# Three buffers in place of two for the split queries between two attention layers

## Chip, cores and metric

The kernel runs on one core of one Trainium2 chip, as one program of 22310 instructions on five engines. TensorE (PE in the profile, its weight loads PEld) multiplies, VectorE (DVE), ScalarE (ACT) and GpSimd (POOL) do elementwise work, SyncE (SP) issues nearly all DMAs. The metric is the device time of one execution in microseconds, the median of several; lower is better.

## What is computed

Two transformer layers on x of shape 4 x 1024 x 128, in float32:

```python
x = L0_attn_query
xn = _layernorm(x)
x = x + _L0_attn_ref(xn, ...) + _L0_ffn_ref(xn, ...)   # causal attention, 16 heads of 8
xn = _layernorm(x)
x = x + _L1_attn_ref(xn, ...) + _L1_ffn_ref(xn, ...)   # keys strided by 3; 2 of 8 experts
```

What matters here lies between the two attentions. Layer 1 needs q = xn @ Wq.T for all 4096 tokens, and k and v of 342 compressed keys of each of the four batches, where a key is a convolution over three tokens of xn:

```python
kc = conv(x.transpose(0, 2, 1), Wconv, stride 3)
k_tmp = concatenate([x[:, :1, :], kc], axis=1)
q = x @ Wq.T;  k = k_tmp @ Wk.T;  v = k_tmp @ Wv.T
```

The router of the experts (the two best of eight, a sigmoid of xn @ gate_w) is computed in the same stage.

## The kernel before

The program is a row of blocks with a barrier of all engines after each: the first projection, a quantised feed-forward, attention of layer 0, `between_layers` (L1400), attention of layer 1, and the experts. The change lies in `between_layers`, with two places in its neighbours.

Scores are computed in bf16 at float32 accuracy: q and k are each split into three bf16 parts (a head, a middle, a tail) that add up to the float32 value. The tokens go through `between_layers` in eight chunks of 512, n = 0 to 7, two to a batch b = n // 2. For one chunk:

- TensorE turns the normalised rows (`turn_xn`, L1511), ScalarE copies them out of PSUM (`copy_xn`, L1616), TensorE projects them into the bank p_q[n % 2] (`query`, L1518) and computes the router's logits (`route`, L1529).
- ScalarE writes the head (`head_q`, L1622) to q_parts[n % 2][:, 0]; TensorE takes it off the bank (`take_off_q`, L1536); ScalarE writes the middle and, after another take-off, the tail (`rest_q`, L1626). The three parts of a chunk stay in one SBUF buffer, `q1_kept0` for even n and `q1_kept1` for odd n.
- SyncE stores the three parts to DRAM by three DMAs of 128 KB (`store_q1`, L1378, by `store_parts`, L202). Each adds 16 to the semaphore q_stored0 or q_stored1. `head_q(n)` waits at L1621 until the store of chunk n - 2, the last user of its buffer, has landed.

For each batch, once its second chunk is there, TensorE convolves (`convolve`, L1550), ScalarE copies the result (L1632), TensorE projects keys and values (`keys_values`, L1560 and L1564), and ScalarE splits the keys likewise: `head_k_copy_v` (L1639, L1642, L1646) and `rest_k` (L1651). The keys have one buffer, `k1_kept`: `head_k_copy_v(b)` waits at L1638 for the store of batch b - 1.

The order on each engine is written out by hand, in ten steps i = 0 to 9 (L1582 on TensorE, L1657 on ScalarE, L1770 on VectorE). ScalarE's step i holds, in this order: the copy of xn of chunk i; for even i from 2 on, the router's sigmoid; the middle of chunk i - 1; for even i, the copy of the convolution of batch i/2 - 1; for odd i from 3 on, the middle of that batch's keys; the head of chunk i; the tail of chunk i - 1; for even i, the head of the keys and the copies of v; for odd i, the tail of the keys. An engine runs its list strictly in order, so a wait holds back all that is listed behind it.

SyncE's list (L1470) is: stores of chunks 0, 1, keys 0, chunk 2, then a wait for keys 0 and chunks 0 and 1 in DRAM (L1480 to L1482) and half of the operand loads of head group 0 for the next attention (`load_operands`, L213 to L217, six or seven DMAs), store of chunk 3, the other half, keys 1, chunks 4 and 5, first half of group 1, keys 2, chunk 6, second half of group 1. The stores of chunk 7 and keys 3 are issued at the start of the next attention (L1015, L1016), which then waits for all of them (L1018, L1019).

At the end of the stage TensorE ranks the tokens of each expert (`rank`, 33 matmuls, L1573 and L1577), behind all else on its list, and VectorE computes from it the place of each token (`place_tokens`, L1734 to L1767). Then comes the barrier, at L1407.

The semaphores of COUNTS (L74) are each raised by one at the start of the program, by TensorE (`prime`, L114, called at L466 to L468).

Of the kernel before, what the change touches and what calls it, by code (L numbers as in the profile page):

```python
# [23 lines left out]
ACT = mybir.ActivationFunctionType  # L24
F32 = mybir.dt.float32
BF16 = mybir.dt.bfloat16
# [5 lines left out]
P = 128  # L32
B, T, E = 4, 1024, 128
H, D = 16, 8
TILES = B * T // P
CHUNK = 512
CHUNKS = B * T // CHUNK
# [9 lines left out]
PARTS = 3  # L47
# [14 lines left out]
START = 1  # L62
# [20 lines left out]
        exp_done unseen_zeroed pv_done v_staged o_copied inverse_done""",  # L83
    "between": """
        o_turned ot_copied projected x_added stats_done moment_steps root_steps xn_ready xn_turned xnt_copied
        q_projected heads_done rests_done middles_done tails_done q_stored0 q_stored1 logits_done conv_done conv_copied
        k_projected k_heads_done k_rests_done k_middles_done k_tails_done k_stored v_projected v_copied
        router_steps sigmoid_done""",
    "plan": """
# [98 lines left out]
Q_ORDER, K_ORDER = range(PARTS), range(PARTS - 1, -1, -1)  # L188
# [5 lines left out]
STORES = 16 * PARTS  # L194


def store_parts(sp, where, order, parts, first, count, stored):


    for row, part in enumerate(order):  # L200
        dst = where[:, row, :, :, bass.ds(first, count)].rearrange("g d a t -> g (d a) t")
        sp.dma_start(dst, parts[:, part, :]).then_inc(stored, 16)  # L202
# [714 lines left out]
def counted_before(layer):  # L917

    geo = Geometry(0)
    units = B * GROUPS  # L920
    uses = sum(what in BANK_USES for what, *_ in geo.order())
    layer0 = dict(banks_filled=uses, banks_read=uses, split_steps=units * geo.split, maxima_stored=16 * units, scores_t_ready=2 * units * geo.S,
                  exp_done=2 * units * geo.S, unseen_zeroed=2 * units * len(geo.masked), pv_done=units * geo.S,
                  v_staged=units, o_copied=units, inverse_done=units)
    return {name: START + layer * count for name, count in layer0.items()}
# [13 lines left out]
def attention(nc, io, sb, dram, layer):  # L939
# [4 lines left out]
    with ExitStack() as ctx:  # L944
# [16 lines left out]
        s, since = sb["counts"]["attention"], counted_before(layer)  # L961
# [23 lines left out]
        def read(use):  # L985

            return since["banks_read"] + use + 1

        def raw_load(sp, b, i):

            sp.wait_ge(e["cut_done"], START + 2 * (BATCH_CUTS * b + max(0, i - 1)))
            sp.dma_start(raw[i % 2][:, :], io["wraw"][b * BATCH_CUTS + i, :, :])\
                .then_inc(sb["raw_in"][i % 2], 16)

        def cut_store(sp, b, i):

            sp.wait_ge(e["cut_done"], START + 2 * (BATCH_CUTS * b + i + 1))
            where = dram["weights"][b * BATCH_CUTS + i, :, :]
            sp.dma_start(where, parts[i % 2][:, :, :].rearrange("p a h -> p (a h)").bitcast(F32)).then_inc(e[f"cut_stored{i % 2}"], 16)
# [12 lines left out]
        @block.sync  # L1012
        def _(sp):
            if layer == 1:
                store_q1(sp, sb, dram, B - 1, 1)  # L1015
                store_k1(sp, sb, dram, B - 1)  # L1016
                for par in range(2):
                    sp.wait_ge(sb["counts"]["between"][f"q_stored{par}"], START + STORES * CHUNKS // 2)  # L1018
                sp.wait_ge(sb["counts"]["between"]["k_stored"], START + STORES * B)  # L1019
            use = 0  # L1020
            for what, n, k, part in order:
                if what == "end" and layer == 0 and n < (B - 1) * GROUPS:
                    b, ends = n // GROUPS, n % GROUPS * 2 + k
                    if 2 <= ends < 2 + BATCH_CUTS:
                        cut_store(sp, b, ends - 2)
                    for i in {0: (0, 1)}.get(ends, (ends,)):
                        if i < BATCH_CUTS and ends != 1:
                            raw_load(sp, b, i)
                if what == "turn_max":
                    sp.wait_ge(s["banks_read"], read(use))  # L1030

                    sp.dma_start(sb["qp"][n % GROUPS][KROWS:FIRST, :, :].rearrange("r j t -> r (j t)"), top_rows[:, :])                        .then_inc(s["maxima_stored"], 16)
                    if layer == 1 and n + 2 < GROUPS:
                        load_operands(sp, sb, dram, layer, geo.keys, 0, n + 2)
                    if layer == 0 and n == B * GROUPS - 1:
                        sp.wait_ge(drawn, 1 + DRAWS * TILES_DRAWN)
                        for g in range(GROUPS):
                            for rows, after in ((sb["kp"][g][FIRST:CROWS, :, 0:KEYS1], after_k),
                                                (sb["qp"][g][FIRST:CROWS, :, :], after_q)):
                                sp.dma_start(rows, after[FIRST:CROWS, :].unsqueeze(1).broadcast_to(list(rows.shape)))\  # L1040
                                    .then_inc(sb["loaded"][g], 16)
                if what == "next_load":
                    sp.wait_ge(s["scores_t_ready"], since["scores_t_ready"] + 2 * S * (n + 1))
                    load_operands(sp, sb, dram, layer, geo.keys, n // GROUPS + 1, n % GROUPS)
                use += what in BANK_USES
            if layer == 1:
                load_shared(sp, io, sb, dram)
            else:
                for g in range(GROUPS):
                    sp.wait_ge(sb["loaded"][g], 16 * (LOADS * B + 2 * LAID))  # L1050
# [327 lines left out]
def store_q1(sp, sb, dram, b, c):  # L1378

    s = sb["counts"]["between"]  # L1380
    sp.wait_ge(s["tails_done"], START + 2 * b + c + 1)
    store_parts(sp, dram["q1"], Q_ORDER, sb["q1_parts"][c], b * T + c * CHUNK, CHUNK, s[f"q_stored{c}"])


def store_k1(sp, sb, dram, b):

    s = sb["counts"]["between"]
    sp.wait_ge(s["k_tails_done"], START + b + 1)
    store_parts(sp, dram["k1"], K_ORDER, sb["k1_parts"], b * KEYS1, KEYS1, s["k_stored"])
# [10 lines left out]
def between_layers(nc, sb, dram):  # L1400
# [6 lines left out]
    with ExitStack() as ctx:  # L1407
        def tmp(name, shape, dt=F32):
            return ctx.enter_context(nc.sbuf_tensor("b_" + name, shape, dt))

        def bank(name):
            return ctx.enter_context(nc.psum_tensor("b_" + name, [P, 512], F32))

        o_t, kct = tmp("o_t", [P, CHUNK]), tmp("kct", [P, KEYS1])
        q_parts, k_parts = sb["q1_parts"], sb["k1_parts"]
        stats, var, mtmp = tmp("stats", [P, TILES, 6]), tmp("var", [P, TILES]), tmp("mtmp", [P, TILES])
        mean, rstd = sb["mean"], sb["rstd"]
# [10 lines left out]
        p_q = [bank(f"pq{i}") for i in range(2)]  # L1428
        routed = p_v[:, KT * P:KT * P + BT * EXPERTS]
        s = sb["counts"]["between"]  # L1430
# [39 lines left out]
        @block.sync  # L1470
        def _(sp):
            load_behind = {2: (0, 0), 3: (0, 1), 5: (1, 0), 6: (1, 1)}
            for b in range(B):
                for c in range(2):
                    n = 2 * b + c
                    if n < CHUNKS - 1:
                        store_q1(sp, sb, dram, b, c)
                    if n in load_behind:
                        if n == min(load_behind):
                            sp.wait_ge(s["k_stored"], START + STORES)  # L1480
                            for par in range(2):
                                sp.wait_ge(s[f"q_stored{par}"], START + STORES)  # L1482
                        g, odd = load_behind[n]
                        load_operands(sp, sb, dram, 1, KEYS1, 0, g, [odd])
                    if c and b < B - 1:
                        store_k1(sp, sb, dram, b)

        @block.tensor
        def _(pe):
# [43 lines left out]

            def take_off_q(n, part, copied):
                pe.wait_ge(s[copied], START + n + 1)
                pe.matmul(p_q[n % 2][:, :], sb["minus_identb"][:, :], q_parts[n % 2][:, part, :], start=False, stop=True,  # L1536
                          skip_group_check=True).then_inc(s["rests_done"], 1)

            def take_off_k(b, part, copied):
# [67 lines left out]
        def _(act):  # L1607
# [9 lines left out]

            def head_q(n):
                act.wait_ge(s["q_projected"], START + n + 1)
                if n >= 2:  # L1620
                    act.wait_ge(s[f"q_stored{n % 2}"], START + STORES * (n // 2))  # L1621
                act.activation(q_parts[n % 2][:, 0, :], p_q[n % 2][:, :], ACT.Copy).then_inc(s["heads_done"], 1)  # L1622

            def rest_q(n, part, copied):
                act.wait_ge(s["rests_done"], START + 2 * n + part)
                act.activation(q_parts[n % 2][:, part, :], p_q[n % 2][:, :], ACT.Copy).then_inc(s[copied], 1)  # L1626

            def copy_convolved(b):
                act.wait_ge(s["conv_done"], START + b + 1)
# [661 lines left out]
```

## Time and profile before

| what | value |
| --- | --- |
| median of 3 runs | 1206.17 us (1204.74 to 1207.23) |
| the profiled execution's own time | 1203.1 us |
| its span (first to last instruction) | 1201.4 us |
| mean granted TensorE clock | 0.955 of 2.4 GHz |
| busy: TensorE matmul, VectorE, ScalarE, GpSimd | 90%, 77%, 60%, 39% of the span |
| `between_layers` in the trace | 681.5 to 748.5 us |
| TensorE's and ScalarE's busy time in it | 53.26 us and 28.53 us of 67.00 us |

The busy share of an engine is an average over stages with different limits; the times below are microseconds from the start of the span. A matmul's end is modelled, so back-to-back matmuls overlap in the rows. SPq is SyncE's queue, with the time that issuing took.

### The profile page before, as it was taken

Reading aid. Unit: us, or ns where it says so; the run is one execution under the profiler, and the core shown is the slowest. Engines: PE = TensorE matmul, PEld = TensorE weight load, DVE = VectorE, ACT = ScalarE, POOL = GpSimd, SP = SyncE. Lnnn points to the kernel's source line nnn. Section 1 sums busy time; section 2 is a strip of 40 time slices with the busy share of each in tenths; the row PEclk is TensorE's granted clock in tenths of the full one; section 3 lists DMA queues with packets and bytes.
Section 4 is the critical chain, followed back from the end, with each engine's and each line's share of the span. In section 5 each row is a group of like instructions: output and inputs, shape, how many; then the busy total and the mean of one; then the engine's idle time right before and its main releaser. Section 6 shows DMA issues by size and latency. Waiting matters only on the chain. (4 is left out here: it accounts for less than half of the span.)

```text
span 1201.4 us, 22310 instructions
## 1 busy us (share of the span) xinstructions
PE 1078.3 (90%) x7591; PEld 595.4 (50%) x7598; DVE 930.1 (77%) x1984; ACT 724.4 (60%) x1110; POOL 471.8 (39%) x809
## 2 busy tenths in 40 slices
PE   4767878999999999999999886999999879999997
PEld 2335664333334344333334464444444358888874
DVE  7979997878888888888887353788878546777776
ACT  3647641466666666666666553466666657778761
POOL 7101221133323333332554320476776712566630
PEclk9988997799999999999999887699999989999999
DMA  5322592011211222122101022222222263677452
GB/s 141 97 89 65 113 147 31 19 54 55 72 63 56 82 72 74 55 84 71 57 5 35 1 78 83 66 62 67 68 62 68 68 198 120 200 243 243 157 133 78
DMA packets 99953, 106.10 MB, mean 88 GB/s; under 512 B 21505, under 2 KB 77334, under 8 KB 99776
## 3 DMA queue, kind: packets, MB, share of 16 engines
q1 hardware_dynamic: 93904, 95.65, 29.8%
q0 software_dynamic: 4992, 8.48, 2.1%
q8 instruction: 62, 1.02, 0.4%
q10 hardware_dynamic: 944, 0.54, 0.2%
q14 instruction: 51, 0.42, 0.1%
HBM read 65.20 MB, written 38.45 MB: 86 GB/s over the span
## 5 line engine op out<-in xcount | busy, mean ns | idle before, releaser
L1256 ACT ACTIVATE a_probs<-a_pst 128x1024 f32<-128x1024 f32 (+4 forms) x544 | 411.9, 808 | 206.8 <-PE a_pst L1200 199.4
L1279 DVE TENSOR_REDUCE a_tops<-a_ps 128x1 f32<-128x512 f32 (+9 forms) x624 | 338.2, 589 | 71.1 <-PE a_ps L1154 68.8
L1098 POOL TENSOR_SCALAR_AFFINE_SELECT a_probs<-a_probs 128x256 f32<-128x256 f32 (+3 forms) x384 | 180.2, 481 | 331.2 <-ACT a_probs L1256 326.8
L1154 PE MATMUL a_ps<-kp,qp 96*128 96x256 bf16 (+10 forms) x2112 | 291.0, 253 | 8.8 <-PEq L1407 4.5
L1200 PE MATMUL a_pst<-qp,kp 98*128 98x512 bf16 (+4 forms) x1088 | 260.8, 332 | 17.7 <-ACT a_probs L1256 12.7
L1154 PEld LDWEIGHTS a_ps<-kp,qp 96*128 96x128 bf16 (+1 forms) x2112 | 140.2, 99 | 214.2 <-DVE a_tops L1279 100.9
L1219 PE MATMUL a_po<-a_probs,vh 128*32 128x512 f32 (+4 forms) x2176 | 229.6, 498 | 12.1 <-POOL a_probs L1098 11.3
L1279 DVE TENSOR_REDUCE a_tops_lead<-a_ps 128x1 f32<-128x512 f32 x256 | 165.1, 685 | 19.1 <-PE a_ps L1154 18.3
L1200 PEld LDWEIGHTS a_pst<-qp,kp 98*128 98x128 bf16 (+1 forms) x1088 | 83.4, 99 | 113.5 <-ACT a_probs L1256 64.8
L1911 POOL DMA_INDIRECT chosen_rows<-e_slot_y,e_slot_x x92 | 93.3, 1014 | 96.9 <-DVE e_slot_y L2131 75.1
L2119 DVE TENSOR_TENSOR e_tails<-e_hidden,e_heads 128x512 fp32r<-128x512 f32 x124 | 86.0, 694 | 39.8 <-ACT e_heads L2053 37.6
L1219 PEld LDWEIGHTS a_po<-a_probs,vh 128*32 128x32 f32 (+1 forms) x2176 | 44.8, 108 | 77.6 <-issue 66.9
L2046 ACT ACTIVATE e_hidden<-e_pup,e_slot_b 128x512 f32<-128x512 f32 x92 | 63.2, 687 | 25.6 <-PE e_pup L1924 23.5
L159 POOL TENSOR_TENSOR f_hq<-f_v,f_sc 128x704 f32<-128x704 f32 x16 | 22.8, 1422 | 120.4 <-DVE f_v L739 113.2
L1110 POOL DMA_INDIRECT slot_rows<-rows,slots x64 | 63.4, 990 | 14.2 <-issue 9.7
L1264 ACT ACTIVATE a_o_raw<-a_po 128x512 f32<-128x512 f32 x32 | 19.1, 598 | 63.7 <-PE a_po L1219 63.7
L625 PE MATMUL f_pg<-wg,big 128*128 128x352 f32 x64 | 27.9, 521 | 16.5 <-DVE f_h L720 15.6
L2117 DVE CAST e_heads<-e_hidden 128x512 fp32r<-128x512 f32 x62 | 26.8, 433 | 18.7 <-ACT e_hidden L2046 18.0
L2053 ACT ACTIVATE e_heads<-e_hidden 128x512 fp32r<-128x512 f32 x62 | 39.2, 632 | 2.0
L1924 PE MATMUL e_pdn<-e_tails,e_slot_w 128*128 128x512 f32 x92 | 36.0, 391 | 0.0
L1922 PE MATMUL e_pdn<-e_heads,e_slot_w 128*128 128x512 f32 x92 | 35.9, 390 | 0.0
L1923 PE MATMUL e_pdn<-e_heads,e_slot_w 128*128 128x512 f32 x92 | 35.9, 390 | 0.0
(330 smaller groups left out, 1513.2 us busy)
## 6 DMA issues: line engine op xcount, KB each, us to landing
e_slot_w<-weight_parts SPq DMA_DIRECT2D x23, 1024.0 KB
qp<-q_parts SPq DMA_DIRECT2D x64, 96.0 KB
slot_rows<-empty_row SPq DMA_DIRECT2D x4, 1495.0 KB, 26.6
e_slot_x<-slot_rows SPq DMA_DIRECT2D x23, 260.0 KB, 3.2
a_raw<-in_wraw SPq DMA_DIRECT2D x18, 256.0 KB, 3.9
weight_parts<-first_rows SPq DMA_DIRECT2D x9, 512.0 KB, 4.4
weight_parts<-a_cut SPq DMA_DIRECT2D x9, 512.0 KB, 3.0
qp<-q_parts SPq DMA_DIRECT2D x64, 64.0 KB
```

The source lines that it names most:

```text
L1098: pool.affine_select(out=seen, in_=seen, compare_op=ALU.is_ge, fill=0.0, base=m0, pattern=[[0, 2], [1, mw]], channel_multiplier=-1 if laye ...
L1110: pool.indirect_dma_start(dram["slots"], bass.IndirectOffsetOnAxis(sb["slots"][:, choice, t:t + 1], 0), sb["rows"][:, t, :], None, bounds_ ...
L1154: last = pe.matmul(bank[:, i * room + at:i * room + to], sb["qp"][slot][0:rows, j, f["qt"] * P:(f["qt"] + 1) * P], sb["kp"][slot][0:rows, ...
L1200: last = pe.matmul(p_st[half][0:st["rows"], i, off:CHUNK], sb["kp"][slot][0:FIRST, half, st["kt"] * P:st["kt"] * P + st["rows"]], sb["qp"] ...
L1219: last = pe.matmul(p_o[VW * j:VW * (j + 1), st["off"]:CHUNK], sb["vh"][n % 2][0:st["rows"], st["kt"], j, v0:v0 + VW], probs[local % RING][ ...
L1256: act.activation(probs[local % RING][0:st["rows"], 2 * part:2 * part + 2, st["off"]:CHUNK], p_st[part][0:st["rows"], :, st["off"]:CHUNK], ...
L1279: dve.tensor_reduce(out, scores, AX.X, ALU.max).then_inc(s["banks_read"], 1)
L1911: pool.indirect_dma_start(dram["chosen"], bass.IndirectOffsetOnAxis(slot_x[r % XR][:, t, E:E + 1].bitcast(U32), 0), slot_y[r % YR][:, t, : ...
L1924: return pe.matmul(out_, w_h, m_tail, start=False, stop=stop, skip_group_check=True)
L2046: act.activation(hidden[m % RR][:, :], p_up[m % UR][:, :], ACT.Gelu, bias=biases(j)[:, k:k + 1])\
L2053: act.activation(heads[m % HR][:, :], hidden[m % RR][:, :], ACT.Copy).then_inc(s["heads_act"], 1)
L2119: dve.tensor_tensor(tails[m % HR][:, :], hidden[m % RR][:, :], heads[m % HR][:, :].bitcast(F32), ALU.subtract)\
```

## The change

Chunk n keeps its parts in buffer n % 3. There is a third buffer of [128, 3, 512] in bf16, 3 KB per partition, allocated within `between_layers`, and a third semaphore, q_stored2. `head_q(n)` waits, from n = 3 on, for the store of chunk n - 3. SyncE waits for both stores from the third buffer at the end of its list in `between_layers`, and the next attention waits for three stores of each of the other two. The PSUM banks p_q stay two, the keys' buffer stays one, and no order is changed.

```diff
-        q_projected heads_done rests_done middles_done tails_done q_stored0 q_stored1 logits_done conv_done conv_copied
+        q_projected heads_done rests_done middles_done tails_done q_stored0 q_stored1 q_stored2 logits_done conv_done conv_copied
@@ attention, sync
-                for par in range(2):
-                    sp.wait_ge(sb["counts"]["between"][f"q_stored{par}"], START + STORES * CHUNKS // 2)
+                for i in range(2):
+                    sp.wait_ge(sb["counts"]["between"][f"q_stored{i}"], START + STORES * len(range(i, CHUNKS, 3)))
@@ store_q1
-    store_parts(sp, dram["q1"], Q_ORDER, sb["q1_parts"][c], b * T + c * CHUNK, CHUNK, s[f"q_stored{c}"])
+    store_parts(sp, dram["q1"], Q_ORDER, sb["q1_parts"][(2 * b + c) % 3], b * T + c * CHUNK, CHUNK,
+                s[f"q_stored{(2 * b + c) % 3}"])
@@ between_layers
+        sb["q1_parts"] = sb["q1_parts"][0:2] + [tmp("q_kept2", [P, PARTS, CHUNK], BF16)]
@@ between_layers, sync
+            sp.wait_ge(s["q_stored2"], START + STORES * len(range(2, CHUNKS, 3)))
@@ between_layers, tensor
-                pe.matmul(p_q[n % 2][:, :], sb["minus_identb"][:, :], q_parts[n % 2][:, part, :], start=False, stop=True,
+                pe.matmul(p_q[n % 2][:, :], sb["minus_identb"][:, :], q_parts[n % 3][:, part, :], start=False, stop=True,
@@ between_layers, scalar
-                if n >= 2:
-                    act.wait_ge(s[f"q_stored{n % 2}"], START + STORES * (n // 2))
-                act.activation(q_parts[n % 2][:, 0, :], p_q[n % 2][:, :], ACT.Copy).then_inc(s["heads_done"], 1)
+                if n >= 3:
+                    act.wait_ge(s[f"q_stored{n % 3}"], START + STORES * (n // 3))
+                act.activation(q_parts[n % 3][:, 0, :], p_q[n % 2][:, :], ACT.Copy).then_inc(s["heads_done"], 1)
...
-                act.activation(q_parts[n % 2][:, part, :], p_q[n % 2][:, :], ACT.Copy).then_inc(s[copied], 1)
+                act.activation(q_parts[n % 3][:, part, :], p_q[n % 2][:, :], ACT.Copy).then_inc(s[copied], 1)
```

## Rows read from the trace of the kernel before

**Rows 1.** ScalarE's waits, 681.5 to 748.5 us: us in total, times, longest
```profile
ACT q_kept L1622 <- DMA q_parts<-q_kept: 14.6, 5, 4.2
ACT k_kept L1639 <- DMA k_parts<-k_kept: 1.1, 1, 1.1
```

**Rows 2.** Timeline of VectorE at the stage's end: start, duration, instruction, idle before
```profile
744.16 0.17 DVE L1741 TENSOR_SCALAR b_counted<-b_py 128x8 int32<-128x8 f32 x1 [5.77 <-PE b_py L1577]
...
748.06 0.20 DVE L1767 CAST slots<-b_slot_f 128x64 uint32<-128x64 f32 x1
```

**Rows 3.** Timeline of ScalarE in the stage
```profile
712.34 0.60 ACT L1622 ACTIVATE q_kept<-b_pq 128x512 bf16<-128x512 f32 x1 [2.93 <-DMA q_parts<-q_kept]
...
728.12 0.60 ACT L1622 ACTIVATE q_kept<-b_pq 128x512 bf16<-128x512 f32 x1 [4.25 <-DMA q_parts<-q_kept]
728.61 0.59 ACT L1626 ACTIVATE q_kept<-b_pq 128x512 bf16<-128x512 f32 x1
729.09 0.46 ACT L1639 ACTIVATE k_kept<-b_pk 128x342 bf16<-128x342 f32 x1
...
733.62 0.60 ACT L1622 ACTIVATE q_kept<-b_pq 128x512 bf16<-128x512 f32 x1 [2.32 <-DMA q_parts<-q_kept]
...
734.59 0.47 ACT L1651 ACTIVATE k_kept<-b_pk 128x342 bf16<-128x342 f32 x1
...
740.43 0.46 ACT L1639 ACTIVATE k_kept<-b_pk 128x342 bf16<-128x342 f32 x1 [1.08 <-DMA k_parts<-k_kept]
```

**Rows 4.** Timeline of SyncE's queue in the stage: start, time of issuing, DMAs
```profile
705.95 1.79 SPq L202 DMA_DIRECT2D k_parts<-k_kept  x3
...
710.48 0.78 SPq L213 DMA_DIRECT2D qp<-q_parts  x1
...
714.84 1.82 SPq L202 DMA_DIRECT2D q_parts<-q_kept  x3
716.70 0.78 SPq L213 DMA_DIRECT2D qp<-q_parts  x1
...
721.53 1.83 SPq L202 DMA_DIRECT2D k_parts<-k_kept  x3
...
723.41 1.79 SPq L202 DMA_DIRECT2D q_parts<-q_kept  x3
...
729.23 1.79 SPq L202 DMA_DIRECT2D q_parts<-q_kept  x3
731.07 0.79 SPq L213 DMA_DIRECT2D qp<-q_parts  x1
...
735.45 1.82 SPq L202 DMA_DIRECT2D k_parts<-k_kept  x3
...
743.51 0.41 SPq L217 DMA_DIRECT2D qp<-no_maxima  x1
```

**Rows 5.** Timeline of TensorE in the last third of the stage
```profile
730.52 1.12 PE L1518 MATMUL b_pq<-big,wq 128*128 128x512 f32 x2 [0.60 <-ACT big L1616]
...
732.60 0.59 PE L1536 MATMUL b_pq<-q_kept,minus_identb 128*128 128x512 bf16 x1
...
734.66 3.62 PE L1550 MATMUL b_pc<-big,wconv 128*128 128x341 f32 x6
...
738.92 0.84 PE L1560 MATMUL b_pk<-b_kct,wk 128*128 128x342 f32 x2 [0.21 <-ACT b_kct L1633]
739.60 0.83 PE L1564 MATMUL b_pv<-wv,b_kct 128*128 128x128 f32 x6
...
742.07 2.05 PE L1577 MATMUL b_py<-hot_sum,ones 128*128 128x256 bf16 x32
```

**Rows 6.** Windows: us, busy time (instructions) of PE, PEld, DVE, ACT, POOL, PE clock, DMA share, GB/s
```profile
732.00:738.80 6.80, 5.91 (x14) 2.86 (x14) 3.22 (x33) 2.54 (x8) 0.00 (x0) 0.50 0.35 101
738.80:749.00 10.20, 4.57 (x59) 3.82 (x60) 3.92 (x15) 2.79 (x8) 0.45 (x3) 1.00 0.23 65
...
749.00:769.50 20.50, 19.61 (x134) 9.53 (x131) 16.61 (x39) 5.46 (x7) 5.25 (x10) 0.50 0.24 64
769.50:790.00 20.50, 19.48 (x221) 9.90 (x219) 15.18 (x36) 13.57 (x19) 14.77 (x23) 1.00 0.26 65
```

**Rows 7.** Timeline of TensorE at the program's start
```profile
12.89 1.09 PE L419 MATMUL n_pxn<-ident,n_xn 128*128 128x128 f32 x4 [12.89 <-DVE n_xn L382]
```

## The prediction, made before the changed kernel was run

> **What bounds the kernel now.** The program is a row of stages with barriers, so only the stage with the edit is read. The first view is that of the waits, for ScalarE in this stage [rows 1]: before five of the eight heads of queries it sits idle until the DMA that empties its buffer has landed, 14.6 us in all, and once, for 1.1 us, until the keys' buffer is empty. That is what the change works on. But 14.6 us of waits are not 14.6 us of time. The second view is VectorE's timeline at the stage's end [rows 2]: the barrier comes behind the placing of tokens, which ends at 748.26 and starts when TensorE's ranking is done. The ranking is last on TensorE's list, behind the take-offs of the last keys. Followed back on ScalarE [rows 3], these hang on the head of keys 3 at 740.43, which waited for the store of keys 2 to land. So the stage's end hangs on a DMA, and the third view is SyncE's queue [rows 4], which is where the store of keys 2 comes from: it was issued at 735.45, behind six loads that had been issued from 731.07 on without a gap, and these behind the store of chunk 5 at 729.23.
>
> In that queue there is one real pause. From 710.48 to 725.20 (723.41 + 1.79) SyncE issues without one: five groups (loads, chunk 3, loads, keys 1, chunk 4) each begin where the one before ends. From 725.20 to 729.23 it waits, 4.03 us, for the tail of chunk 5, which ScalarE wrote at 728.61 to 729.20 because the head of chunk 6, listed before it, had waited 4.25 us for a buffer [rows 3]. From 729.23 on it is again without a pause, to the end at 743.92.
>
> **Part 1: the waits for the query buffers go.** With three buffers head n asks for the store of chunk n - 3. The store of chunk 3 was issued at 714.84 to 716.66, and a store's wait ends 2.74 to 3.16 us after its last issue (keys 0: 707.74 to the load at 710.48; chunk 4: 725.20 to 728.12; keys 2: 737.27 to 740.43) [rows 3, 4]. So head 6 finds its buffer free at about 719.6, and head 7, which asks for chunk 4, at about 728.1. Neither is late any more: the tail of chunk 5 would be ready by 729.20 - 4.25 = 724.95 even if nothing ahead of it moved, and head 7 comes 728.8 at the earliest (below). Of the 14.6 us on ScalarE, most comes off its own idle time, and the heads of chunks 3 to 6 move forward more and more. That is worth nothing in itself, because SyncE's issues from 710.48 to 725.20 don't move: the keys 0 must first land, and their own store at 705.95 waits for little that the change touches.
>
> **Part 2: what SyncE gains.** The store of chunk 5 follows that of chunk 4 at once, at 725.25 in place of 729.23. The six loads behind it follow, and the store of keys 2 can be issued at 735.45 - 3.98 = 731.47. It lands after 3.16 us of waiting behind its last issue, as now, so head of keys 3 starts at 740.43 - 3.98 = 736.45.
>
> **Part 3: what is late next.** Two other conditions must hold for that. First, the tail of keys 2 must be written by 731.47. It hangs on the head of keys 2, and this now waits for the store of keys 1, whose issue at 721.53 to 723.36 has not moved. It lands at 723.36 + 2.74 to 3.16, at 726.1 to 726.5; the same head starts at 729.09 today. This is a new wait on ScalarE of about 3.5 us, with the copies of v, the copy of chunk 7 and the head of chunk 7 queued behind it, and TensorE's query of chunk 7 waiting for those. From that head to the keys' tail, without today's 2.32 us of waiting for a buffer, the rows give: query of chunk 7 ends 731.64, its head can start at 731.70, the take-off of chunk 6 ends at 733.19, its tail then takes its 0.48 us step, and the keys' tail 0.47: 734.15, which is 5.1 us after 729.09 [rows 3, 5]. So the tail is ready at 731.2 to 731.6, and the keys' store issued at 731.47 to 731.6: it just meets SyncE. Second, TensorE must have the projected keys and values by 736.45. The convolution of batch 3 begins behind the take-off of the head of chunk 7; that head starts 2.6 us after the head of keys 2, at 728.8, in place of 733.62, so the convolution may begin behind TensorE's take-off of the keys' middle, at about 730.9 in place of 734.66, and its end and the values, 739.60 + 0.83 = 740.43 now, come at 736.65 [rows 5]. Both paths arrive together with the store, within 0.2 us.
>
> The sum of the stage is thus 3.98 us less 0.1 for these near meetings: 3.9 us off its end. Take-offs, ranking and placing follow at their present lengths [rows 2, 5]. SyncE's list ends at 743.92 - 3.98 = 739.94, ahead of the barrier at about 744.6.
>
> **Part 4: what is added.** One semaphore is raised once more by TensorE at the start, where its first matmul comes only after 12.89 us of waiting for VectorE [rows 7]: nothing; without that cover an instruction of this kind would cost less than the smallest row here, 0.17 us. SyncE's wait for the third buffer at the end asks for chunk 5, landed by 730, ten microseconds before: nothing. The waits of the next attention count the same stores, with the same last one. The 3 KB move later buffers of the stage; no row prices an address, so I take zero, with 0.17 us, the smallest row, per affected step as a bound either way on the one path, which gives about 0.5 us.
>
> **Against which time.** The sum against the profiled execution is 1203.1 - 3.9 = 1199.2 us. That execution was 3.1 us under the median of the runs, so against the median it is 1206.17 - 3.9 = 1202.3 us. A measurement of this kernel can tell about 0.2%, 2.4 us, from no change.
>
> **A rule against the trace.** Around the edit the granted clock is not one value: 0.50 (1.2 GHz) from 732.0 to 738.8, 1.00 (2.4 GHz) until 749.0, and 0.50 again to 769.5 in the next attention [rows 6]. Before the second fall TensorE was busy only 4.57 us of 10.20. The Trainium skill, TensorE: Matmul & The Clock Gate, section "What's actually happening", has it that the throttled state is the default and activity releases it. By that rule a moved gap can move the low stretches, and the time could come out otherwise than by my sum; the rivals 2 and 3 price that from rows.
>
> **Rivals.** (1) *The keys' buffer takes the place of the queries'.* If the store of keys 1 lands late, the whole tail of the stage is late with it. It must have landed by 729.09 today, since that head shows no wait of its own; at that worst the keys' tail comes at 734.15, the store of keys 2 at 734.2, and 1.25 us are left: 1204.9 us. It decides against a gain of 2.4 us once keys 1 land after 727.95, 4.6 us behind their last issue. Against it speak the three landings of 2.74 to 3.16 us; for it, that store stands behind seven loads. Chance 0.09.
>
> (2) *The low clock falls on the ranking.* Today it returns at 738.8, just before the last values and the ranking. If the low stretch is moved onto them, the ranking's 2.05 us and the keys' 0.84 and values' 0.83 us [rows 5] can at most double, so up to 3.7 us is given back, and 1206.0 us is left. From 1.5 us given back on, the gain is under 2.4 us. For it: that stretch of TensorE is thin (4.57 us busy of 10.2) [rows 6]. Against it: TensorE's work from 730.9 to 736.65 is as dense as today's. Chance 0.10. Rivals 1 and 2 both end within 0.2%.
>
> (3) *Slower: the next attention stays at 1.2 GHz longer.* The first 20.5 us of it are at 0.50 with TensorE busy 19.61 us, the next 20.5 us at 1.00 with 19.48 us [rows 6]. Each microsecond more at half clock loses at most half a microsecond of work. If the low stretch were as long again, 10.25 us would be lost: 1206.17 - 3.9 + 10.25 = 1212.5 us. It turns the sign (slower by over 2.4 us) at 12.6 us more of low clock. The order of work there isn't changed, only its offset by 3.9 us. Chance 0.07. The same shift can shorten the stretch, which would add to the gain.
>
> (4) *The third buffer does nothing*, since another condition held the heads: 1206.2 us. Against it: the wait's releaser is the store itself five times [rows 1], and SyncE's pause ends with the tail. Chance 0.03.
>
> **How the numbers follow.** The forecast, 3.9 us faster, has 0.71. Its own range: the landing (2.74 or 3.16 us), 0.5 us for addresses, and a median of runs that spread over 2.5 us, make 1200.5 to 1204.0. The range for 8 in 10 goes up to rivals 1 and 2, to 1206.2, and down to 1199.0 for a shorter low stretch. Faster 0.71, within 0.2% 0.22 (rivals 1, 2 and 4), slower 0.07.
>
> **What would show it.** Right: the stage ends 3.5 to 4.3 us earlier; ScalarE's waits for q_parts fall from 14.6 us to under 1; a new wait of 3 to 4 us before the second-to-last head of keys; SyncE's queue has no pause between the stores of chunks 4 and 5; the store of keys 2 starts near 731.5. Wrong: that store starts after 733, or the stage is shorter and the next attention longer by as much, or the low clock lies on the ranking.

## The result: 3 us faster, where 3.9 us was forecast

| | median | lowest to highest | executions |
| --- | --- | --- | --- |
| kernel before | 1206.95 us | 1204.73 to 1208.61 us | 9 |
| changed kernel | 1203.78 us | 1201.97 to 1205.88 us | 9 |

The ratio is 0.9976 with a 95% interval of 0.9967 to 0.9986, so 1.7 to 4.0 us faster, 2.9 us in the middle. The interval holds the 3.9 us of the forecast too, so the times alone do not show a shortfall; the queue and the length of the stage do, below. The profiled execution of the changed kernel took 1203.82 us with a span of 1202.1 us, longer than the 1201.4 us of the profile before. The two profiles alone would say that nothing was gained; why they mislead is shown below. The stage itself became 3.15 us shorter between them (67.01 and 63.86 us).

ScalarE's waits in the changed kernel from 681.5 to 745 us (us in total, times, longest), against [rows 1]:

```profile
ACT q_kept L1625 <- PE b_pq L1521: 7.5, 6, 2.2
...
ACT k_kept L1642 <- DMA k_parts<-k_kept: 5.2, 2, 4.7
```

The wait for the queries' stores, 14.6 us before, is gone from the list. The wait for the keys' stores has grown from 1.1 to 5.2 us. ScalarE's timeline shows where, against [rows 3]:

```profile
725.82 0.46 ACT L1642 ACTIVATE k_kept<-b_pk 128x342 bf16<-128x342 f32 x1 [4.65 <-DMA k_parts<-k_kept]
...
729.36 0.60 ACT L1625 ACTIVATE q_kept<-b_pq 128x512 bf16<-128x512 f32 x1 [1.33 <-PE b_pq L1521]
...
731.80 0.45 ACT L1654 ACTIVATE k_kept<-b_pk 128x342 bf16<-128x342 f32 x1
...
736.97 0.46 ACT L1642 ACTIVATE k_kept<-b_pk 128x342 bf16<-128x342 f32 x1 [0.51 <-DMA k_parts<-k_kept]
```

SyncE's queue in the changed kernel, against [rows 4]:

```profile
720.86 1.83 SPq L202 DMA_DIRECT2D k_parts<-k_kept  x3
722.74 1.80 SPq L202 DMA_DIRECT2D q_parts<-q_kept  x3
724.58 1.88 SPq L202 DMA_DIRECT2D q_parts<-b_q_kept  x3
726.50 0.79 SPq L213 DMA_DIRECT2D qp<-q_parts  x1
...
730.17 0.68 SPq L215 DMA_DIRECT2D kp<-k_parts  x1
732.28 1.82 SPq L202 DMA_DIRECT2D k_parts<-k_kept  x3
...
740.35 0.42 SPq L217 DMA_DIRECT2D qp<-no_maxima  x1
```

The pause of 4.03 us between the stores of chunks 4 and 5 is gone (724.54 to 724.58). A shorter one has appeared: the last load was issued by 730.85, the store of keys 2 only at 732.28, 1.43 us later, because its tail was written at 731.80 to 732.25. TensorE shows why the tail was late, against [rows 5]:

```profile
726.33 0.47 PE L1544 MATMUL b_pk<-k_kept,minus_identb 128*128 128x342 bf16 x1 [3.91 <-ACT k_kept L1642]
727.25 2.08 PE L1521 MATMUL b_pq<-big,wq 128*128 128x512 f32 x2 [0.45 <-ACT big L1619]
729.12 1.71 PE L1532 MATMUL b_pv<-gw,big 128*128 128x8 f32 x8
...
731.77 3.62 PE L1553 MATMUL b_pc<-big,wconv 128*128 128x341 f32 x6
...
738.78 2.05 PE L1580 MATMUL b_py<-hot_sum,ones 128*128 128x256 bf16 x32
```

The query of chunk 7 took 2.08 us where it took 1.12 us before, and the logits behind it 1.71 us. In front of them TensorE was idle for 3.91 us, and at about 725.5, near the end of that idle time, the granted clock fell to 0.50 (1.2 GHz), where it stayed until 735.7 (windows of the changed kernel, columns as in [rows 6]):

```profile
722.40:725.70 3.30, 0.02 (x1) 0.00 (x0) 0.00 (x0) 0.00 (x0) 0.00 (x0) 0.96 0.49 135
725.70:735.20 9.50, 8.42 (x21) 4.90 (x21) 2.86 (x31) 4.38 (x11) 0.00 (x0) 0.50 0.38 111
735.20:745.00 9.80, 4.71 (x45) 3.37 (x43) 4.14 (x17) 2.83 (x8) 0.00 (x0) 0.97 0.25 75
```

In the first 3.30 us no engine computes: ScalarE waits for the store of keys 1, and the work of the others hangs on ScalarE. The placing of tokens then ends like this, against [rows 2]:

```profile
744.77 0.19 DVE L1770 CAST slots<-b_slot_f 128x64 uint32<-128x64 f32 x1
```

That is 744.96 in place of 748.26 us.

### The profile page after: what moved, and what is told of

It is laid out like the page before. It is cut to its first block and busy times, and to the rows that moved or that the text cites. A ratio compares the mean times of both kernels' runs of the same rounds, so it can differ in the third digit from the quotient of the medians.

```text
span 1202.1 us, 22318 instructions
## 1 busy us (share of the span) xinstructions
PE 1079.0 (90%) x7598; PEld 594.8 (49%) x7598; DVE 931.5 (77%) x1984; ACT 725.0 (60%) x1110; POOL 471.6 (39%) x809
```

## The experiments

**The yardstick.** Two distances proved much steadier than the whole time: from the start of the store of keys 1 to that of keys 2 in SyncE's queue, and from there to the end of the placing of tokens. The table has them for every profile taken (us; the stage runs from TensorE's first matmul in it to its first in attention 1). Each ratio below is against executions of the kernel before that were made beside it, with medians of 1202.53 to 1202.97 us.

| kernel (profile) | keys 1 to keys 2 | keys 2 to placed | stage | attention 1 |
| --- | --- | --- | --- | --- |
| before | 13.92 | 12.81 | 67.01 | 221.96 |
| before, second | 14.20 | 12.72 | 66.28 | 221.33 |
| changed | 11.42 | 12.68 | 63.86 | 225.84 |
| changed, second | 11.76 | 12.71 | 64.14 | 221.87 |
| changed, third | 10.37 | 12.70 | 63.19 | 224.35 |
| `only6` | 11.60 | 12.79 | 64.19 | 221.87 |
| `allbut67` | 14.12 | 12.49 | 65.97 | 224.15 |
| `filler` | 9.94 | 12.98 | 62.65 | 221.36 |
| `k_two_q_two` | 14.13 | 12.34 | 66.64 | 222.10 |
| `k_first` | not comparable | 13.30 | 61.19 | 221.68 |
| `k_two` | 9.94 | 11.34 | 58.71 | 222.00 |
| `q_four_k_two` | 9.94 | 7.27 | 58.80 | 221.33 |

**Which of the waits counted.** Two kernels split the third buffer's effect, by giving the chunks other buffers. The first frees chunk 6 alone:

```diff
+Q_AT = [0, 1, 0, 1, 0, 1, 2, 1]
...
-                act.activation(q_parts[n % 3][:, 0, :], p_q[n % 2][:, :], ACT.Copy).then_inc(s["heads_done"], 1)
+                act.activation(q_parts[Q_AT[n]][:, 0, :], p_q[n % 2][:, :], ACT.Copy).then_inc(s["heads_done"], 1)
```

The waits, the stores and the take-offs use Q_AT in the same way. The heads of chunks 3, 4, 5 and 7 wait for the store two chunks back, as before.

> The third buffer is used by chunk 6 alone (buffers 0 1 0 1 0 1 2 1): the heads of chunks 3, 4 and 5 wait as in the kernel before. Theory (SyncE's pause before the store of chunk 5 is the whole gain): head 6 starts at about 725.0 without a wait, the store of chunk 5 moves from 729.2 to about 726.3, the store of keys 2 from 735.45 to 732.5 to 733.0, and the time falls by 2.5 to 3.0 us. Rival (each microsecond of ScalarE's 14.6 us of waits is worth the same): 4.25 of 14.6 us, so 0.9 us faster.

Measured: ratio 0.9978 (0.9965 to 0.9990), 2.6 us faster. SyncE's queue in this kernel:

```profile
721.67 1.80 SPq L204 DMA_DIRECT2D q_parts<-q_kept  x3
...
726.15 0.79 SPq L215 DMA_DIRECT2D qp<-q_parts  x1
...
731.40 1.82 SPq L204 DMA_DIRECT2D k_parts<-k_kept  x3
```

The store of chunk 4 ends at 723.47, that of chunk 5 takes the 1.8 us ahead of the loads at 726.15, so 0.8 us is left of the pause of 4.03 us, and the store of keys 2 comes at 731.40, although ScalarE still waits 10.8 us for queries' stores here. One freed head out of five makes nearly the whole gain. From its stage's start, keys 2 come at 51.1 us, as expected (732.5 to 733.0 is 50.9 to 51.4 us). The second kernel does the opposite:

```diff
+Q_AT = [2, 1, 0, 2, 1, 0, 1, 0]
```

Here the heads of chunks 6 and 7 wait for the store two chunks back, as before.

> Three buffers in the order 2 1 0 2 1 0 1 0: the heads of chunks 3, 4 and 5 no longer wait, those of 6 and 7 wait for the store two chunks back as in the kernel before. Theory (the gain is SyncE's pause): head 6 still waits for the store of chunk 4, which can move only by the 0.7 us by which keys 0 come earlier; 0.7 us faster than before. Rival (waits of ScalarE are worth their length): 8.0 of 14.6 us of waits are gone, 1.75 us faster.

Measured: ratio 0.9999 (0.9990 to 1.0008), no change. Its head of chunk 6 collects what the three others no longer wait:

```profile
728.68 0.60 ACT L1627 ACTIVATE q_kept<-b_pq 128x512 bf16<-128x512 f32 x1 [7.90 <-DMA q_parts<-q_kept]
```

It waits 7.90 us in place of 4.25 us, for the same store of chunk 4, and nothing is won. The three heads that had waited 8.0 us in sum are free, but the time is not: most of it returns in front of chunk 6, and ScalarE waits 10.4 us for queries' stores in all. That is 4.2 us less than the 14.6 us of before, for no gain, where `only6` waits 3.8 us less for 2.6 us. Equal lengths have unequal prices, so the rival that prices ScalarE's waits by their length falls; its 1.75 us also lie outside the interval, which ends at 1.2 us faster. The 0.7 us that the theory still allowed lie inside it and are neither shown nor excluded. They rested on times from the start of the span, which differ between executions by as much (in the second profile of before the keys 1 store starts 39.04 us into the stage, in three of the changed kernel 39.44, 39.35 and 39.81 us).

**Why 3.9 us was not reached.** The idle time of TensorE was filled with matmuls that nobody reads, everything else left as it is. The wait ahead of them keeps them from overwriting their bank before its last reader is done:

```diff
+                if i == CHUNKS - 1:
+                    pe.wait_ge(s["x_added"], START + late(CHUNKS))
+                    for _ in range(16):
+                        pe.matmul(p_y[:, :], sb["identb"][:, :], q_parts[(i - 1) % 3][:, 0, :], start=True, stop=True,
+                                  skip_group_check=True)
                 if lagged(i) is not None:
                     take_off_k(lagged(i), 0, "k_heads_done")
```

> The changed kernel with 16 matmuls of 128x512 in bf16 added on TensorE ahead of the take-off of the head of keys 2, where it stood idle 3.9 us; they write a bank that nothing reads before it is written again. Theory (the gain fell short of 3.9 us because this idle time took the clock to 1.2 GHz, which made the query and the logits of chunk 7 1.4 us slower, so the tail of keys 2 came 1.4 us after SyncE was ready): granted clock stays 1.00 from 722 to 732 us, the store of keys 2 starts at 730.9 in place of 732.3, the stage ends 1.2 to 1.4 us earlier than in the changed kernel. Rival (the clock does not matter; the loads and landings set the store): the stage ends within 0.3 us of the changed kernel's 745.0.

Measured: ratio 0.9963 (0.9948 to 0.9977), 4.5 us faster than before. The stage took 62.65 us, against 63.86, 64.14 and 63.19 us in the three profiles of the changed kernel. TensorE, SyncE and the window of this kernel:

```profile
722.51 3.62 PE L1595 MATMUL b_py<-q_kept,identb 128*128 128x512 bf16 x16
726.56 0.32 PE L1544 MATMUL b_pk<-k_kept,minus_identb 128*128 128x342 bf16 x1 [0.43 <-ACT k_kept L1647]
727.48 1.13 PE L1521 MATMUL b_pq<-big,wq 128*128 128x512 f32 x2 [0.60 <-ACT big L1624]
728.44 0.95 PE L1532 MATMUL b_pv<-gw,big 128*128 128x8 f32 x8
```

```profile
731.06 1.82 SPq L202 DMA_DIRECT2D k_parts<-k_kept  x3
```

```profile
720.00:732.00 12.00, 10.97 (x54) 6.36 (x55) 2.50 (x25) 5.37 (x13) 0.00 (x0) 1.00 0.40 116
```

The granted clock stays at 1.00 (2.4 GHz), the query takes 1.13 us and the logits 0.95 us, and the store of keys 2 starts 9.94 us after that of keys 1: exactly what SyncE needs for the nine stores and six loads in that stretch, and the 13.92 - 3.98 us of the forecast. More work, a shorter stage. Part of what the queue gained is lost behind it: the head of keys 3 waits until 3.33 us behind the last issue of keys 2, where it was 2.87 us in the changed kernel, and the placing comes 12.98 us after that store. The intervals of the timed ratios of this kernel and the changed one overlap, and it has one profile; the distance in the queue and the stage's length carry the verdict. The kernel with four and two buffers, below, reaches the same 9.94 us without added work: TensorE has no such wait there, and the clock stays at 1.00 from 700 to 738 us. The Trainium skill, TensorE: Matmul & The Clock Gate, section "What's actually happening", has the throttled state as the default that activity releases; by that rule, the trace agrees (1.00 with the added work, 0.50 without it).

**The keys' buffer.** If the single buffer of the keys is what is late next, a second one should free the rest; alone, without the third buffer of queries, it should do little.

```diff
+        sb["k1_parts"] = [tmp("k_kept1", [P, PARTS, KEYS1], BF16), sb["k1_parts"]]
...
-                if b:
-                    act.wait_ge(s["k_stored"], START + STORES * b)
+                if b >= 2:
+                    act.wait_ge(s[f"k_stored{b % 2}"], START + STORES * (b // 2))
```

> The changed kernel with two buffers for the split keys as well. Theory (the keys' one buffer is the new limit: the head of keys 2 waits 4.65 us for the store of keys 1, and all of step 7 behind it): the head of keys 2 starts at about 721.5 in place of 725.8, TensorE keeps its clock, SyncE issues without a pause from 709.8 on and ends at about 739.4, which now ends the stage together with the placing of tokens at about 739: 5.3 us earlier than the changed kernel, 8 to 9 us under the kernel before. Rival (SyncE's stores and TensorE's chain set the end, the buffer does not): within 1 us of the changed kernel.

> The kernel before with a second buffer for the keys and two for the queries. Theory (the queries' waits come first there, the keys' wait of 1.08 us only at the end): 0.5 to 1.1 us faster than before. Rival (either buffer alone would do): 3 us faster or more.

Measured: with two query buffers 0.9996 (0.9988 to 1.0005), no change; with three 0.9961 (0.9947 to 0.9974), 4.7 us faster than before. The head of keys 2 no longer waits, but the stage moved only in part by the mechanism that was named. From the store of keys 1 to the first matmul of attention 1 it takes 21.60 us, against 24.42 us in the changed kernel: 2.8 us. The other half of the 5.2 us by which its stage is shorter lies before that store, where the granted clock returned earlier (at 688.5 us, against 694.7 us), and was not asked for. And a new wait stands in its place, before the head of chunk 7:

```profile
724.39 0.60 ACT L1628 ACTIVATE q_kept<-b_pq 128x512 bf16<-128x512 f32 x1 [4.27 <-DMA q_parts<-q_kept]
```

That is the store of chunk 4 again, queued behind seven loads and keys 1. TensorE's clock fell in this wait too (0.50 from 722.7 to 729.5 us), against the expectation, but keys 2 were early enough: their store still comes 9.94 us after keys 1. A second profile of this kernel was taken, with the stage at 58.29 us and attention 1 at 223.24 us:

> The kernel with three buffers for the queries and two for the keys, unchanged, for a second profile. Its first profile had attention 1 at 222.0 us and a span of 1191.8 us, 4 us under its median, while its stage was 8 us shorter than before. Theory A (attention 1 takes 222 or 226 us by the execution): this profile shows either, with the stage at 58.7 us again. Theory B (only the changed kernel's own profile is odd): 222 us again.

**Order in place of memory.** The keys' stores ahead of the loads, with one buffer for them:

```diff
+                    if c and 0 < b < B - 1:
+                        store_k1(sp, sb, dram, b)
                     if n in load_behind:
...
-                    if c and b < B - 1:
+                    if c and b == 0:
                         store_k1(sp, sb, dram, b)
```

> The changed kernel with one change to SyncE's order: the stores of keys 1 and keys 2 are issued ahead of the half loads of operands that stood before them, the keys' buffer stays one. Theory (the head of keys 2 waits because its store stands behind seven loads in the queue): the store of keys 1 starts at 716.1 in place of 720.9, the head of keys 2 waits for nothing and starts at about 721.0 to 721.5, the head of keys 3 at about 731.2; the stage ends at about 739.5, 5 us earlier than the changed kernel. Rival (the loads are what the next attention needs first, and delaying them costs it): the stage ends earlier but the next attention starts with a wait of up to 2 us for its operands.

Measured: ratio 0.9952 (0.9937 to 0.9967), 5.8 us faster than before, 1196.00 us against 1202.97 us in the median. The stage is 61.19 us long, 2.7 us shorter than in the changed kernel's profile where 5 was expected. Counted from the stage's start, the store of keys 1 begins at 34.7 us in place of 39.4 us and the head of keys 2 at 40.6 us in place of 44.4 us, as meant. But the store of chunk 4 has kept its place behind the loads (41.4 us, 41.3 us in the changed kernel), the head of chunk 7, which is there sooner, waits 3.29 us for it, and SyncE then waits 2.4 us, from 725.50 to 727.91, for the tail of keys 2. The next attention did not start with a wait for operands (its first 23 us show no wait for a load, and it is 221.68 us long): the rival falls. A second profile had the stage at 61.02 us and attention 1 at 221.80 us:

> The kernel with the keys' stores ahead of the loads, unchanged, for a second profile: stage 61.2 us again; attention 1 at 222 or 226 us by theory A, at 222 us by theory B.

**The limit.** Four buffers for queries (2 3 0 1 2 3 0 1) and two for keys:

> Four buffers for the queries and two for the keys. In the kernel with three and two the head of chunk 7 still waits 4.27 us for the store of chunk 4, which stands behind seven loads and the store of keys 1, and TensorE's clock falls. Theory (SyncE's list of DMAs is then the only limit of the stage): no head waits for a store, SyncE issues without a pause as with three and two and ends 55.5 us after the stage's start, the placing of tokens ends before it, the stage is 56 us long in place of 58.7 us, and the time is 2.5 to 2.8 us under that of three and two. Rival (TensorE's and ScalarE's chain is the limit): stage within 0.5 us of 58.7 us.

Measured: ratio 0.9938 (0.9920 to 0.9956), 7.5 us faster than before, the best of all, 1194.83 us in the median. No head waits for a store. SyncE and VectorE at the end of its stage:

```profile
730.92 1.82 SPq L204 DMA_DIRECT2D k_parts<-b_k_kept  x3
...
738.99 0.41 SPq L219 DMA_DIRECT2D qp<-no_maxima  x1
```

```profile
737.99 0.20 DVE L1776 CAST slots<-b_slot_f 128x64 uint32<-128x64 f32 x1
```

The placing ends at 738.19, SyncE's last issue at 739.40: the bound has changed to the queue. From the store of keys 1 (720.98) to there SyncE needs 18.42 us without a pause, as it does with three and two buffers, where the placing came 2.9 us behind it. The stage as a whole, 58.80 us, is no shorter than that of `k_two`, against the expectation of 56 us: its store of keys 1 comes 39.8 us into the stage, that of `k_two` 37.1 us, with the earlier clock named above. So the rival's number for the stage came out, but not its reason. The timed ratio is 2.8 us under that of `k_two`, as expected, but the two intervals overlap and the runs were made on different chips.

**What the profiles of before and after hid.** The same kernels again:

> The kernel before, unchanged, for a second profile. In the profile of before the sixteen turns of the maxima in attention 1 stand mostly 12.7 us apart, in that of the changed kernel 13.0 us, so the changed one lost 3.9 us there that the median of its runs does not show. Theory A: the two paces are a property of an execution, not of the change: then this profile may show either pace, and its span is about 1201.5 us at the fast one, 1205 us at the slow one. Theory B: the change causes the slower pace: then this profile has 12.7 us again, and a span near 1201.5 us. Either way the stage between the attentions ends its placing at 748.2 to 748.4 us.

> The changed kernel, unchanged, for a second profile. Theory A (pace of attention 1 is a property of the execution): the turns of the maxima may stand 12.7 or 13.0 us apart. Theory B (the change causes the slower pace): 13.0 us again. The stage between the attentions ends its placing at about 745.0 us either way.

> The changed kernel, unchanged, for a third profile: stage 64.0 us again; attention 1 at 222 or 226 us by theory A.

Measured: before again, stage 66.28 us and span 1200.2 us; changed again, 64.14 us and 1197.9 us; changed a third time, 63.19 us and 1198.4 us. Averages of the stage are 66.65 us (two) and 63.73 us (three), a difference of 2.9 us, the same as the ratio gives. The placing ends at 744.93 us in the second profile of the changed kernel, as expected, and at 747.40 us in that of before, 0.8 us earlier than expected. The first profile of the changed kernel lost 3.9 us in attention 1. Two turns of the maxima of neighbouring units there, and the same two in the second profile:

```profile
845.59 0.24 PE L1163 MATMUL a_ps<-identb,a_top_parts 128*64 128x128 bf16 x1
858.56 0.24 PE L1163 MATMUL a_ps<-identb,a_top_parts 128*64 128x128 bf16 x1
```

```profile
843.72 0.24 PE L1163 MATMUL a_ps<-identb,a_top_parts 128*64 128x128 bf16 x1
856.41 0.24 PE L1163 MATMUL a_ps<-identb,a_top_parts 128*64 128x128 bf16 x1
```

12.97 us in one, 12.69 us in the other, of one and the same program. Theory A holds so far: the pace can differ between executions of one program. Whether the change makes the slow one more frequent, three profiles of it can't tell.

Not tried: the filling matmuls together with a second buffer for the keys, and the last loads of SyncE moved behind the barrier, which might take some of its 18.42 us off.

## Why the prediction was right, and where it was not

- **What bounds the stage**: right. The end hangs on the store of keys 2, and the distance from it to the placed tokens is 12.68 to 12.81 us in every profile of before and of the changed kernel. ScalarE's 14.6 us of waits are not time: `allbut67` frees the heads that had waited 8.0 us of them and wins nothing. The second path of part 3 is as near as it was said to be: in the third profile the head of keys 3 is released by TensorE's projection of the keys and not by the store.
- **Part 1 and part 2**: right. Only the head of chunk 6 matters, by way of the tail of chunk 5 and SyncE's pause; `only6` shows it. The store of chunk 5 came 1.84 us after that of chunk 4 began, as forecast.
- **Part 3, the landing of keys 1**: right in mechanism and size. Forecast 2.74 to 3.16 us behind its last issue, measured 725.82 - 722.69 = 3.13 us; it was 3.47 and 2.97 us in the second and third profile, once outside the range. The new wait was put at 3.5 us and is 4.65 us, since ScalarE reached it earlier; the length of that wait has no price of its own.
- **Part 3, from the head of keys 2 to its tail**: this is the step that failed. The sum took 5.1 us from the rows of before, with a query of 1.12 us at the full clock and logits of 1.27 us; measured are 725.82 to 732.25, 6.4 us. The wait that I had forecast empties TensorE, and the clock falls at its end (in the third profile 1.9 us behind it). The consequence of my own step, idle time on TensorE right before the work that the sum needs, was not carried into the durations of that work. SyncE's wait for that tail is 1.4 us in this profile (730.85 to 732.28), 1.9 us in the second, 0.3 us of it from the later landing, and 0.5 us in the third, where the clock fell 1.4 us later, at 726.9, so that the query still took 1.19 us. `filler` gives it back.
- **The sum**: 3.9 us forecast, 2.9 us measured, in the times and in the mean lengths of the stage. From keys 1 to keys 2 the forecast took off 3.98 us; the means of the table give 2.9 us. The range, 1199.0 to 1206.2 us, holds 1203.78 us.
- **The low clock, rival 2**: half right. It was priced on the ranking, which ran at the full clock in 2.05 us as before; it fell on the query and the logits of chunk 7, where it could delay the store. Its price belonged at the place of the idle time that the change itself makes.
- **Rival 1**, a late landing: did not happen (3.47 us at most, where 4.6 us were needed). **Rival 3**, a longer stay at 1.2 GHz at the start of attention 1: not seen. The low stretch there ended at 766.4 us, 21.1 us after that attention's first matmul, against 20.9 us before.
- **Against which time**: the first profile of the changed kernel had the longest attention 1 of all, that of before (221.96 us) a usual one, as ten of the fourteen have. Why the profiled execution of before was 3.1 us under its median stays open. The sum against the median gave 1202.3 us, 1.5 us under the measured one, of which 0.8 us is the median of before, 1206.95 us in nine runs where it was 1206.17 us in three.

## What to carry to other kernels

Here a wait for a buffer on a compute engine was worth what it delayed in the queue that ends the stage: find the pause in that queue, and free only the wait that makes it. When a freed wait brings the next one forward, look at what TensorE does during that next wait; if it stands idle there, reckon the work behind it at the lower clock. And compare stages, not spans, where a later stage of the same program varies by more than the change is worth.

## What was not expected of the hardware

- Attention 1 took between 221.3 and 225.8 us in fourteen profiles of programs whose instructions for it are the same in the same order, while the experts' stage took 230.6 to 231.2 us. Two forms show: units about 12.97 us apart in place of 12.69 us through most of the stage (the changed kernel's first profile), and a granted clock of 0.77 over the stage's last 30 us (`allbut67`) and 0.80 (the changed kernel's third profile), against 0.95 in the profile of before; these two attentions are 2.2 and 2.4 us longer than that one. What sets either was not found. None of the three profiles with two query buffers showed it and four of the eleven others did; whether a kernel can make it more frequent stays open. The median of `k_two`, 4.7 us better where its stage is some 8 us shorter, leaves room for that.
- With sixteen matmuls whose result is thrown away the stage was 0.5 to 1.5 us shorter, in the one profile taken, than in the three of the changed kernel.
- The granted clock at the start of the stage had a mean of 0.50 to 0.64 over the window 681.5 to 697.0 us in twelve profiles, and 0.78 in both of `k_two`, whose store of keys 1 comes up to 2.7 us earlier in the stage than in the changed kernel. Whether that comes with the kernel or by chance is open.
